# Attention in a three-stage block: the groups written out, weighted sums spread evenly, 3 key tiles on VectorE, TensorE's weighted sum ahead of the scores

## The reference

```python
x = L0_attn_x                                   # 1 x 4096 x 256, float32
x = x + 0.5 * _L0_ffn_ref(_layernorm(x), ...)   # routed experts, 4 of 32 per token, and a shared one
x = x + _L0_attn_ref(_layernorm(x), ...)
x = x + 0.5 * _L0_ffn_ref(_layernorm(x), ...)   # the same weights again

def _L0_attn_ref(x, qkv_w, qkv_b, proj_w, proj_b):          # H = 16 heads of HD = 16
    qkv = jnp.einsum('bsd,ed->bse', x, qkv_w) + qkv_b
    qkv = qkv.reshape(b, s, 3, H, HD)
    q, k, v = ...                                           # each b x H x s x HD
    scores = jnp.einsum('bhqe,bhke->bhqk', q, k) * scale    # scale = 1 / sqrt(HD)
    attn = jax.nn.softmax(scores, axis=-1)
    out = jnp.einsum('bhqk,bhke->bhqe', attn, v)
    out = jnp.transpose(out, (0, 2, 1, 3)).reshape(b, s, d)
    return jnp.einsum('bsd,ed->bse', out, proj_w) + proj_b

def _L0_ffn_ref(x, Wg, W1, W2, W3, Ws1, Ws2, Ws3):
    scores = jax.nn.softmax(xf @ Wg, axis=-1)
    weights, indices = jax.lax.top_k(scores, TOP_K)
    ...                                                     # per expert: gather, swiglu, weight, add
    return y + swiglu(xf, Ws1, Ws2, Ws3)
```

## Time and profile before

| | |
|---|---|
| median of 3 runs | 2959.52 us |
| the profiled execution: its own time | 2960.84 us |
| its span | 2958.9 us |
| mean granted TensorE clock | 0.96 of full |
| busy: TensorE, ScalarE, VectorE, GpSimd | 2651.8, 2235.4, 2172.9, 715.7 us |

### The profile page before, as it was taken

How to read it: one execution, slowest core, us unless ns; L and a number is a source line. 1 busy time by engine, 2 the same in 40 slices (tenths; PEclk the granted TensorE clock), 3 DMA queues, 4 the chain that set the end, 5 groups by cost and what they waited for, 6 DMA issues and landing times. The chain is left out here.

```text
span 2958.9 us, 58436 instructions
## 1 busy us (share of the span) xinstructions
PE 2651.8 (90%) x17801; PEld 1088.0 (37%) x17803; DVE 2172.9 (73%) x4261; ACT 2235.4 (76%) x3211; POOL 715.7 (24%) x1014
## 2 busy tenths in 40 slices
PE   5799979969999989999989999999999975999971
PEld 5499845511111111111111111111111153899541
DVE  6777758757787877787877886886877868677454
ACT  4644425579999989999999999999999946344320
POOL 1566668520000000000000000000000013666576
PEclk9999989979999999999999999999999995999986
DMA  6555645520010010010010010010001026555644
GB/s 183 153 172 172 159 115 145 138 41 3 5 25 3 5 26 3 5 25 3 5 26 3 5 25 3 5 25 5 3 3 33 3 79 179 164 171 169 117 126 121
DMA packets 132102, 196.00 MB, mean 66 GB/s; under 512 B 22364, under 2 KB 99324, under 8 KB 130428
## 3 DMA queue, kind: packets, MB, share of 16 engines
q1 hardware_dynamic: 104188, 117.00, 14.1%
q0 software_dynamic: 27648, 75.53, 10.6%
HBM read 124.85 MB, written 67.50 MB: 65 GB/s over the span
## 5 line engine op out<-in xcount | busy, mean ns | idle before, releaser
L1714 ACT ACTIVATE RB<-psS 128x1024 f32<-128x1024 f32 x1888 | 1737.0, 1163 | 8.5 <-PE psS L1631 8.3
L1673 PE MATMUL psO<-RB,values 128*32 128x512 f32 x7552 | 1026.5, 607 | 0.0
L1631 PE MATMUL psS<-WE 51*128 51x512 f16 x3776 | 696.6, 387 | 79.3 <-ACT RB L1714 29.3
L1631 PEld LDWEIGHTS psS<-WE 51*128 51x128 f16 x3776 | 168.3, 93 | 1123.1 <-ACT RB L1714 1101.9
L660 POOL DMA_INDIRECT xg<-xn_d,index x320 | 305.4, 954 | 184.6 <-issue 150.5
L1733 DVE TENSOR_SCALAR scaled<-psO 128x512 int32<-128x512 f32 x320 | 218.6, 683 | 170.9 <-PE psO L1631 170.9
L686 PE MATMUL psH<-xgt,chosen 128*128 128x128 f32 x2560 | 341.9, 277 | 0.2 <-DVE xgt L743 0.2
L1578 POOL COPY values<-WE 128x480 f32 x12 | 7.0, 584 | 1300.5 <-PE psO L1673 1300.5
L686 PEld LDWEIGHTS psH<-xgt,chosen 128*128 128x128 f32 x2560 | 314.9, 194 | 0.7 <-issue 0.6
L1760 DVE SCALAR_TENSOR_TENSOR WE<-WE 128x1024 f32<-128x1024 f32 x240 | 287.4, 1216 | 1.6
L1760 DVE SCALAR_TENSOR_TENSOR series<-series,WE 128x1024 f32<-128x1024 f32 x240 | 287.3, 1215 | 1.6
(11 more groups left out here) (243 smaller groups left out, 2960.5 us busy)
## 6 DMA issues: line engine op xcount, KB each, us to landing
pair_d<-ob SPq DMA_DIRECT2D x320, 128.0 KB, 2.2
WE<-part_d SPq DMA_DIRECT2D x84, 128.0 KB
xn_d<-ws SPq DMA_DIRECT2D x64, 128.0 KB, 1.7
WE<-in_W SPq DMA_DIRECT2D x2, 4096.0 KB, 24.0
part_d<-raw SPq DMA_DIRECT2D x32, 256.0 KB, 2.8
xg<-xn_d,index POOLq DMA_INDIRECT x320
RA<-in_x SPq DMA_DIRECT2D x8, 512.0 KB, 7.3
head_d<-sums SPq DMA_DIRECT2D x128, 32.0 KB, 1.6
```

Of the source, the lines that this page charges most:

```text
L1631: return pe.matmul(ps, K[r][rows, kt * P:(kt + 1) * P], Q[r][rows, first:first + BLK], start=True, stop=True)
L1673: last = pe.matmul(psO[g % 2][32 * j:32 * (j + 1), :], values[:, r, j % 2, row, :], weights, start=(kt == 0), stop=(kt == WHOLE[1]))
L1714: act.activation(probs[m % RING], psS[hold(m)][:, :], ACT.Exp, scale=SCALE).then_inc(sem("exped"), 1)
```

## The change

- `attend` is written out: all 32 groups stand one after the other on every engine, with constants in the waits, and `rounds` is gone.
- 58 units of a group go to ScalarE, and 6 to VectorE: the whole key tiles 29, 30 and 31 (`KEPT = KT - 3`). The polynomial has four steps in place of five, and works in pairs of units; there are 12 reads in place of 10, of which the first 4 of a group are made during the group before.
- `weigh_slot` spreads the 32 weighted sums evenly over 58 slots (one in 1.81 slots) with the three of VectorE between the others (`order`), each not before slot 2 kt + 2.
- In a slot TensorE now does W, then S of the unit two ahead, then D.
- `bound_shift` is gone. Its work stands at the end of `combine_project`, where ScalarE computes the shift in two halves and stores it itself, to `shift_d` and into the query operand of the first pair. `attend` no longer loads the first pair's shift, and its first two S stand ahead of the wait for `value_ones`.
- In `route` the wait for the gate weights `wg` moves from the start of TensorE's program to the first gate score.

```diff
-                pe.wait_ge(sem("wg"), 16)
                     pe.wait_ge(sem("xnt_ready"), t + 1)
+                    if t == 0:
+                        pe.wait_ge(sem("wg"), 16)
...
-    bound_shift(nc, sem, sb, pb, ident, env["norms"], env["query_norm"], env["key_norm"], env["key_mean"], env["safe"], shift_d)
-    exact_shift(nc, sem, sb, pb, ident, env["safe"], part_d, shift_d)
+    exact_shift(nc, sem, sb, pb, ident, env["safe"], part_d, shift_d, Q[0])
...
                     sp.dma_start(shift_d[n].rearrange("h (b t) -> h b t", t=BLK),
                                  zero[:, :].unsqueeze(1).to_broadcast([NH, NB, BLK])).then_inc(sem("zeros_out"), 16)
+                    for h in range(2):
+                        sp.dma_start(Q[0][h * HALF_ROWS + SHIFT_ROW + n:h * HALF_ROWS + SHIFT_ROW + n + 1, :]
+                                     .rearrange("h (b t) -> h b t", t=BLK),
+                                     zero[0:1, :].unsqueeze(1).to_broadcast([1, NB, BLK])).then_inc(sem("zeros_out"), 16)
...
-                sp.wait_ge(sem("zeros_out"), 32)
+                sp.wait_ge(sem("zeros_out"), 16 * 6)
+                sp.wait_ge(sem("shift_out"), 16 * 6)
...
+                def shifted(half):
+                    w = slice(half * WIDE, (half + 1) * WIDE)
+                    act.activation(shift[:, w], norms[:, w], ACT.Sqrt, scale=far[:, :]).then_inc(sem("shifts"), 1)
+                    act.wait_ge(sem("shifts"), half + 1)
+                    act.dma_start(shift_d[1][:, w], shift[:, w]).then_inc(sem("shift_out"), 16)
+                    for h in range(2):
+                        at = h * HALF_ROWS + SHIFT_ROW + 1
+                        act.dma_start(Q[0][at:at + 1, w], shift[h:h + 1, w]).then_inc(sem("shift_out"), 16)
+
+                act.wait_ge(sem("norm_kept"), NB)
+                act.wait_ge(f_sem("z_ready"), NT)
+                act.wait_ge(sem("far"), 1)
+                shifted(0)
+                act.wait_ge(sem("far"), 2)
+                act.activation(most[:, :], long[:, :], ACT.Sqrt, scale=far[:, :]).then_inc(sem("bounded"), 1)
+                act.activation(below[:, :], low[:, :], ACT.Sqrt).then_inc(sem("bounded"), 1)
+                shifted(1)
+
...
-def bound_shift(nc, sem, sb, pb, ident, norms, query_norm, key_norm, key_mean, safe, shift_d):
...
-                act.wait_ge(sem("far"), 2)
-                act.activation(most[:, :], long[:, :], ACT.Sqrt, scale=far[:, :]).then_inc(sem("bounded"), 1)
-                act.activation(below[:, :], low[:, :], ACT.Sqrt).then_inc(sem("bounded"), 1)
-                act.activation(shift[:, :], norms, ACT.Sqrt, scale=far[:, :]).then_inc(sem("shifts"), 1)
...
-            @block.sync
-            def _(sp):
-                sp.wait_ge(sem("shifts"), 1)
-                sp.dma_start(shift_d[1], shift[:, :]).then_inc(sem("shift_out"), 16)
-                sp.wait_ge(sem("shift_out"), 16)
...
+    GROUPS = PAIRS * QG
-    SPLIT, WHOLE = 29, (30, 31)
+    KEPT = KT - 3
+    CHUNKS = 2 * KEPT
+    DUETS, DUNITS = 3, 6
+    READS = 2 * DUNITS
+    UNITS = GROUPS * CHUNKS
-    START = 5
-    DIVERT_AT = (10, 12, 14, 16, 19, 22, 26, 30, 34, 42)
-    WEIGH_AT = {kt: KEPT.index((kt, 1)) + LAG for kt in range(SPLIT)}
-    WEIGH_AT.update({SPLIT: 37, 30: 52, 31: CHUNKS + 4})
+    TERMS = (7317.71252, 1325.56323, 38.7851540, 3.73876140)
+    FIRST_DIVERTS = (0, 2, 4, 6)
+    DIVERTS = (5, 8, 11, 14, 17, 21, 25, 29, 34, 38, 42, 46)
+    LATER_DIVERTS = (8, 11, 13, 16, 19, 22, 26, 30, 34, 38, 42, 46)
+    def order(g):
+
+        at = (12, 21, 30) if g == 0 else (7, 18, 29)
+        kts = list(range(KEPT))
+        for n, x in zip(at, range(DUETS)):
+            kts.insert(n, KEPT + x)
+        return kts
+
+    def weigh_slot(g, n):
+
+        kt = order(g)[n]
+        slot = (33 * KT + 10 * n * CHUNKS) // (10 * KT)
+        return max(slot, 2 * kt + LAG) if kt < KEPT else slot
 
     def weighed(g, kt):
 
+    def diverts(g):
+
+        now = [(slot, g, d) for d, slot in enumerate(FIRST_DIVERTS)] if g == 0 else []
+        slots = LATER_DIVERTS if g == 0 else DIVERTS
+        for k, slot in enumerate(slots):
+            if k + 4 < READS:
+                now.append((slot, g, k + 4))
+            elif g + 1 < GROUPS:
+                now.append((slot, g + 1, k + 4 - READS))
+        return now
...
-        def rounds(eng, body):
-            with eng.Fori(0, PAIRS // 2 - 1) as r:
-                body(r, False)
-            body(PAIRS // 2 - 1, True)
...
-                pe.wait_ge(sem("value_ones"), 8)
...
+                def scores(m):
+                    g, i = divmod(m, CHUNKS)
+                    kt, h = divmod(i, 2)
+                    if i == 0 and g == 0:
+                        operands(g)
                     if m >= HELD:
...
+                def divert(g, d):
+                    unit, n = divmod(d, 2)
+                    if d == 0 and g % QG == 0 and g > 0:
+                        operands(g)
+                    if d == 4 and g > 0:
+                        pe.wait_ge(sem("o_out"), g)
+                    if g * READS + d > 0:
+                        pe.wait_ge(sem("d_read"), g * READS + d)
+                    bank = psO[1] if g == 0 else psO[g % 2] if d < 4 else psO[(g + 1) % 2]
+                    score(bank[:, :], g, KEPT + unit // 2, 2 * (unit % 2) + n).then_inc(sem("d_scored"), 1)
+
...
+                    if kt < KEPT:
+                        pe.wait_ge(sem("exped"), g * CHUNKS + 2 * kt + 2)
+                        pe.wait_ge(sem("d_exped"), g * DUNITS + 2 * (kt - KEPT) + 2)
...
-                def slot(r2, m, last):
-                    g, i = m // CHUNKS, m % CHUNKS
-                    if m + LAG < BODY or not last:
-                        scores(r2, m + LAG)
-                    if i in DIVERT_AT:
-                        divert(r2, g, DIVERT_AT.index(i))
-                    for kt in ORDER:
-                        if WEIGH_AT[kt] % CHUNKS == i:
...
+                    scores(m)
+                pe.wait_ge(sem("value_ones"), 8)
+                for g in range(GROUPS):
+                    at = diverts(g)
+                    own = [(weigh_slot(g, n), kt) for n, kt in enumerate(order(g))]
+                    before = [(weigh_slot(g - 1, n) - CHUNKS, kt) for n, kt in enumerate(order(g - 1))] if g else []
+                    for i in range(CHUNKS):
+                        m = g * CHUNKS + i
+                        for slot, kt in before:
+                            if slot == i:
+                                weigh(g - 1, kt)
+                        for slot, kt in own:
+                            if slot == i:
+                                weigh(g, kt)
+                        if m + LAG < UNITS:
+                            scores(m + LAG)
+                        for slot, dg, d in at:
+                            if slot == i:
+                                divert(dg, d)
+                for slot, kt in own:
+                    if slot >= CHUNKS:
+                        weigh(GROUPS - 1, kt)
 
...
+                for m in range(UNITS):
+                    act.wait_ge(sem("scored"), m + 1)
+                    if m >= RING and m % 2 == 0:
+                        g, i = divmod(m - RING, CHUNKS)
+                        act.wait_ge(sem("pv"), weighed(g, i // 2))
+                    act.activation(probs[m % RING], psS[m % HELD][:, :], ACT.Exp, scale=SCALE).then_inc(sem("exped"), 1)
...
+                def opening(g):
+                    for u in range(2):
+                        bits(g, u)
+                    for u in range(2):
+                        squares(g, u)
+                    for u in range(2):
+                        fourths(g, u)
+
+                def duet(g, u, after):
+                    for step in (squares, fourths, sixths, ending):
+                        if after is not None:
+                            read(*after.pop(0))
+                        step(g, u)
+                        step(g, u + 1)
+
+                for pair in range(2):
+                    fill(pair)
+                for d in range(4):
+                    read(0, d)
+                opening(0)
+                for g in range(GROUPS):
+                    if g:
+                        normalise(g - 1)
+                    read(g, 4)
+                    for u in range(2):
+                        sixths(g, u)
+                    read(g, 5)
+                    for u in range(2):
+                        ending(g, u)
+                    read(g, 6)
+                    bits(g, 2)
+                    read(g, 7)
+                    bits(g, 3)
+                    duet(g, 2, [(g, d) for d in range(8, READS)])
+                    for u in (4, 5):
+                        bits(g, u)
+                    more = g + 1 < GROUPS
+                    duet(g, 4, [(g + 1, d) for d in range(4)] if more else None)
+                    if more:
+                        opening(g + 1)
```

(1 more changed line is left out.)

388 lines of the change are left out of this document (124 added, 264 removed).

## The result

The changed kernel takes 2941.0 us (median of 4 runs, 2940.6 to 2942.4) against 2959.7 (2957.3 to 2964.1): ratio 0.9936, 95% interval 0.9919 to 0.9953. That is 18.7 us less. 30.4 were forecast, so some 12 us are missing, and the question is where. The profiled execution has a span of 2938.9 us, 20.0 less than before.

What follows compares the result with a forecast made beforehand. ScalarE's exponentials bound the attention, TensorE close behind. Stream 1703.1 + 27.5 + 3.5 = 1734.1 against 1754.6, 20.5 less; with 6.9, 1.0 and 2.0, 30.4 less: 2929 us. Its own range 2918 to 2940, with rivals 2899 to 2956.

Steps and rivals of the forecast that it cites:

- ScalarE's cadence: Attention: exponentials start 0.9176 us apart where the stream is whole; 1856 of them take 1703.1 us.
- the late S at slots 15, 35 and 55: TensorE in attention: weighted sums put first make scores late by 0.36, 0.36 and 0.14 us; 0.86 a group, 27.5 in all.
- Rival A: Attention: scores are not late, slots being less tight or TensorE running ahead; 2902 us, chance 0.20.
- C: Attention: a weighted sum started from a wait costs over 0.26 us extra, starving ScalarE at all 16 places; 2980 us, chance 0.10.
- E: Attention: VectorE late for slot 5, 15 or 35 beyond its 2 to 3 us; 2961 us at one, chance 0.07.
- D: Written-out attention: the longer program pays for instruction fetching, 4 us per 8 groups, 16 us; 2945 us, chance 0.08.
- The loop: Attention before: 22 us of the stream lost by first units and two loop turns; the turns go, straight code charged nothing.
- The start of group 0: First attention groups: TensorE's lower clock level and waits for value copies starve exponentials; 3.5 us, between 1.3 and 6.
- The seam: Projection to attention: square roots on ScalarE in the projection let `attend` start at 613.0, 3.9 us earlier; 2 to 6.
- The first S: Start of attention: first scores no longer wait for `value_ones` and the shift; 3.28 us becomes about 0.3, 3.0 less.
- The end: After the last exponential: last transpose 1.0 us sooner; next stage no longer waits for `wg`, 2.0 us less.
- VectorE: Attention: at most 1.5 us more work a group, 44.3 busy of 54, hidden under ScalarE.

Runs made afterwards that it cites:

- b: Changed kernel with the scores of the unit two ahead put first in a slot, then diverted scores, then weighted sum: stage 1718.1 us, ratio to before 0.9852.
- c: Changed kernel with the weighted sums of VectorE's three key tiles one slot later (16, 36, 56): stage 1722.8 us, ratio to before 0.9867.
- d: Changed kernel with two diverted scores of a group one slot earlier (13 and 33 for 14 and 34): stage 1737.0 us, ratio to before 0.9911.
- g: Kernel before with its attention loop of three rounds written out, nothing else changed: ratio 0.9929, stage 1732.1 us.
- a: Changed kernel with GpSimd's eight bias additions moved behind the last copy of values, into group 24: stage 1746.8 us, ratio to before 0.9935.
- n: Changed kernel once more, unchanged, as yardstick for other runs: stage 1747.9 us, ratio to before 0.9940.
- l: Changed kernel with scores first in a slot, bias additions one a group and group 0's first reads spread: stage 1707.1 us, ratio to before 0.9820.
- j: Changed kernel with GpSimd's eight bias additions spread, one in each of groups 1 to 8: stage 1739.5 us, ratio to before 0.9899.
- i: Kernel before with only the square roots, bound and first shift rows moved into the projection's last block: ratio 0.9980.
- h: Kernel before with only the router's weights wait moved to first use: last exponential to TensorE's next-stage start 9.66 us, 11.68 before.

## Why the prediction was right, and where it was not

**The steady state: right, term by term.** ScalarE's cadence (0.9176 forecast, 0.9168 measured in b, which is 1.5 us over 1856), the late S at slots 15, 35 and 55 (0.36, 0.36 and 0.14 forecast; 0.37, 0.37 and 0.16 measured from the ends of the exponentials, 0.90 a group against 0.86), their cause (b, c, d) and the price of a W behind a wait (1.00) all hold. Rival A falls, since the gaps are there, and C, since W to S behind a wait costs no more than elsewhere. No W waited for VectorE in a late group: E falls. D falls with the single row of g; the two queues that load instructions moved 3.09 MB after and 3.46 before.

**The loop: right in the sum, in part by luck.** I had read 22 us lost in the stream before, and gave them to the first units and the two turns; written out the stage is 21.5 less, but the turns and the first group are only 18.2 of it. The other 3.4 are in groups inside the loop, where I had not looked, since I took the cadence from groups outside.

**The start of group 0: wrong, and all of the miss.** The step was the "3.5, between the 1.3 of before and 6" for first units. It was 19.7 less the 0.9 that group 0 shares with all groups: 18.8, some 15 more. I had priced TensorE's lower level and the wait for the copies, and these came as priced (0.49, 2.31, 0.48 and 0.29, together 3.57 before the long gap). The sum has no term for the gap of 13.24 and the 1.10 behind it, where TensorE is at its lower level again. I had not looked at what follows when reads start 18 us earlier: 616.78 instead of 634.76. In the kernel before (timelines of GpSimd and VectorE) the first bit operation fell on the end of the additions and took 1.71 us, as the only one:

```profile
619.77 18.63 POOL L1566 TENSOR_TENSOR RA<-RA,WE 128x1024 f32<-128x1024 f32 x8
...
634.76 0.69 DVE L1733 TENSOR_SCALAR scaled<-psO 128x512 int32<-128x512 f32 x1 [12.51 <-PE psO L1631]
...
637.24 1.71 DVE L1739 TENSOR_SCALAR WE<-scaled 128x1024 int32<-128x1024 int32 x1
```

That row could be seen, and a row at 2.5 times its usual length beside another engine's work asks for an explanation. And TensorE's order puts the D of slot 11 before the next W and S, while VectorE's puts the read that it needs behind an opening of 7 us even undisturbed (706.01 to 712.96 in a). The opening starts behind the read for the D of slot 6, and the five slots from there to 11 give it 4.6 us.

The Trainium skill, SBUF — State Buffer, Who interferes with whom, says that VectorE and GpSimd have a pair of SBUF ports in common that one instruction holds to its end while the other waits, and that VectorE takes it for operations with two SBUF inputs beside a GpSimd operation that reads SBUF, and for single-source ones in certain fast modes, but not for one with at most one SBUF input outside these modes. The trace agrees: 2.83 for 0.68 and 6.38 for 2.35, and the read from PSUM, which has no SBUF input, unchanged at 0.68. That one waits for the other in turn is not shown instruction by instruction here; the additions of 4.04 and 5.27 us beside undisturbed steps fit it.

**The seam: right in kind, small.** 3.9 forecast, 3.8 measured. The first S: 3.0 forecast, and the first exponential gained 5.57 - 1.30 = 4.3 from the first memset on, the 3.0 and the table load of 1.28, which ScalarE now does while it waits (611.67 in the kernel after) and not after the first S. The router's weights in the first stage, of which I said that they may give up to 1 and took none, brought 1.5: the last reduction stands at 597.73 instead of 599.19.

```profile
597.73 0.67 DVE L1331 TENSOR_REDUCE key_norm<-psQ 16x1 f32<-16x512 f32 x1
...
611.66 0.48 POOL L1558 MEMSET values<- 128x464 f32 x1 [45.47 <-POOLq L1414]
611.67 1.28 ACT L1686 ACT_TABLE_LOAD   x1 [6.57 <-PEq L1414]
```

**The end: right.** Last exponential (2361.79) to transpose 1.19 us (2.37 before: 1.2 less, 1.0 forecast), and TensorE starts the next stage with its operands (2.0 less forecast, 2.2 measured):

```profile
2362.98 0.72 DVE L1745 STREAM_TRANSPOSE turned_sums<-psO 128x512 f32<-128x512 f32 x1 [12.64 <-PE psO L1651]
...
2370.07 2.04 PE L440 MATMUL psI<-WE 128*128 128x256 f32 x4 [7.16 <-PEq L61]
```

The last 1.3 us, after that start, no run explains; n, the same kernel, takes 569.8 us there against 568.8, so most of it is no more than two executions differ by.

**VectorE: right in the sum, with a slip in the words.** The prediction speaks of two pairs of bit operations more in a group; its sum has two operations, and the windows count 53 instructions where there were 50 (two reads, two bit operations, one step less).

## What to carry to other kernels

A stream at its bound is priced by adding the starts of what one engine must issue between two of its deadlines; that sum was right to 0.02 us a place, and the cure it pointed to (scores first) was worth more than the change it came with. But a steady state says nothing of its first round: when work is moved to start earlier, list what else runs in that time on engines that were "off the path", and follow the first waits through both queues. The bulk job on GpSimd cost 8 to 9 us of the stage in one piece, at the start as in group 24, and nothing that shows in groups 2 to 8 when it was cut into pieces, each released in front of a stretch in which VectorE has time to spare.

## What the runs showed of the hardware

- VectorE's operations within SBUF beside GpSimd's 128x1024 f32 addition: bit operation 0.68 to 2.83 us, two polynomial steps 2.35 to 6.38. Reads from PSUM stay at 0.68.
- The addition itself, each of eight in a row: 2.3 us (18.63 / 8) in the kernel before, where VectorE was idle beside most of them, 2.5 (19.95 / 8) at the start after, 2.9 (23.40 / 8) beside the polynomial. Alone and released during a step: 4.04 (l) and 5.27 (j).
- A turn of the hardware loop around the attention cost between 5.4 and 9.6 us (ScalarE's group at the turn against its neighbours, six turns in three executions), and a group inside the loop lasts 0.16 us more than one outside (54.26, 54.10).
- Two chips reached the first exponential 66 to 84 us later than the third (679 to 687 and 692 to 697 us against 612 to 613 in the kernel after and its variants), and ran the attention's late groups alike.
- ScalarE's table load stands before the wait for the first scores in every program without a loop (611.67 in the kernel after; g: 683.44, with TensorE's queue as releaser) and behind it in the three with the loop (before: 621.23, behind the scores of 620.23; i: 617.09; h: 619.72). That is 1.28 us. Why is not shown: no run tests it by itself.
